# Where VectorE takes the reciprocals of the previous half slot's second side in a chain of four attention layers

## The chip, the core and the metric

The program runs on one core of one Trainium2 chip. TensorE (PE in the rows) multiplies matrices, VectorE (DVE) and ScalarE (ACT) read and write both memories, GpSimd (POOL) works on SBUF, SyncE (SP) issues transfers; each engine runs its own queue in order and waits on semaphores. The metric is the device time of one execution in microseconds, the median of the runs.

## What is computed

Four cross attention layers one after the other on x (8 batches of 128 tokens, 128 channels), with a context of 8 x 128 x 256. Layers 0 and 3 are narrow (16 heads of 8 channels, 4 key heads, an RMS norm ahead of the queries), layers 1 and 2 are wide (16 heads of 64 channels, a column bias on the scores). The reference, cut to what matters:

```python
def narrow(x, cond, wq, wk, wv, wo, norm_w):
    xn = rmsnorm(x, norm_w)
    q = (xn @ wq).reshape(B, T, 16, 8)
    k, v = (cond @ wk).reshape(B, S, 4, 8), (cond @ wv).reshape(B, S, 4, 8)
    ...
    attn = jax.nn.softmax(scores, axis=-1)
    return x + out @ wo

def wide(x, ctx, Wq, Wk, Wv, Wo, bo, ...):
    logits = jnp.einsum('bhqd,bhkd->bhqk', q, k) * scale + col_bias
    probs = jax.nn.softmax(logits, axis=-1)
    ...
    return out @ Wo + bo + x

x = narrow(x); x = wide(x); x = wide(x); x = narrow(x)
```

## The kernel before

**Jobs and half slots.** A job is one layer of one batch: 32 jobs, in the order of `JOBS` (line 73), all four layers for batches 0 to 3 and then for batches 4 to 7. So jobs 0 to 3, 12 to 19 and 28 to 31 are narrow, the others wide. A job has 16 heads in two octets; octet o = 2n + h is half h of job n, and half slot o (`half(n, h)` on each engine) is the turn of each engine's program in which octet o's scores are made. An octet has two sides of four heads, each side one PSUM bank of 128 x 512. There are 64 octets, o = 0 to 63, and a few slots of draining. Each engine's program is unrolled by hand, and only its own order and the semaphores decide when something runs.

**The way of an octet.** TensorE makes the scores of both sides (`scores`, L825 narrow, L836 wide). VectorE's `scores_out(o, side)` (L615) takes each head's column out of PSUM into `probs` and its negated maximum into `negmax`, four heads a side, and signals `scores_read[side]` with the last. ScalarE's `exponentials` (L482) makes the exponentials of the four heads and their row sums and signals `exps_made[side]`. VectorE's `inverse_sums(o, side)` (L622) takes the reciprocals of the four row sums, 128 x 4, and signals `inv_made[side]`. GpSimd's `normalise(o, side)` (L379) multiplies `probs` by them, 128 x 512. One half slot later or more TensorE transposes the side (`transpose_probs(o - 2)` in slot o, L849), VectorE or ScalarE copies the transposes to `probsT` (L626, L499), and TensorE multiplies with the values (`weighted_values`, L870 narrow, L882 wide). Then come the output projection (L900) and the addition to x (L641, L643).

**VectorE's slot o** is, in this order: the addition to x and the mean of squares (odd slots, where due), `scores_out(o, 0)`, `inverse_sums(o - 1, 1)`, `scores_out(o, 1)`, `outputs_out` (L631, L633), `narrow_queries` (L594 and L598, once a narrow job, in even slots there), the copies of octet o - 2's transposes, `inverse_sums(o, 0)`. The reciprocals of octet o's second side thus come one slot late.

**GpSimd's slot o** is `normalise(o, 0)`, `normalise(o, 1)`, and in even slots round narrow jobs, behind these, `narrow_values` (L356), `inverse_root` (L361, the 1/sqrt of the RMS norm of the next narrow job, `inv_rms`), `square` (L373), and `diagonal_keys` (L343) of a job two ahead, at some places with `split_keys` (L328, L331) ahead of it. VectorE's `scores_out(2n, 0)` of a narrow job n waits for `inverse_root(n)` by the semaphore `rms_made`, besides the scores themselves.

**TensorE's slot o**: `scores(o)`, `weighted_values(o - 3)` for a wide job, `transpose_probs(o - 2)`, `weighted_values(o - 3)` for a narrow one, the pieces of the key and value projections that `FILLS` (line 85) gives to the slot (L701 to L703; the last in slot 55), the queries of a job ahead (L788, L796), the mean of squares (L807) and the output projection. Transposes of octet o wait for `pt_read` of octet o - 1.

Of the kernel before, what the change touches and what calls it, by code (L numbers as in the profile page):

```python
# [112 lines left out]
def job(n):  # L113

    return JOBS[n] if 0 <= n < NJOBS else (None, None)


def is_narrow(n):

    return 0 <= n < NJOBS and JOBS[n][0] in NARROW  # L120


def is_wide(n):

    return 0 <= n < NJOBS and JOBS[n][0] not in NARROW
# [7 lines left out]
def scores_bank(o):  # L133

    return "fill" if o >= LAST_FILL + 2 and o % 2 == 1 else "scores"
# [7 lines left out]
def query_half(n):  # L143

    return 2 * n - 3 if n >= 2 and is_narrow(n - 1) else 2 * n - 2


def narrow_index(n):

    return NARROW_JOBS.index(n)  # L150


def build(nc, xT, ctxT, narrow_w, narrow_kv, kv_w, qo_w, small, tokens, outT):
    with ExitStack() as ctx:
# [109 lines left out]
        def valid(o):  # L264

            return 0 <= o < 2 * NJOBS

        def scalar_copy(o):

            return valid(o) and is_narrow(o // 2)  # L270
# [255 lines left out]
        def _(dve):  # L526
# [8 lines left out]
            def norm_weights(n):  # L535

                dve.wait_ge(narrow_q_loaded[n], 16)
                wq = wn[:, NQ + n * REP * STACK:NQ + (n + 1) * REP * STACK]
                nc.vector.tensor_scalar(wq, wq, vec[:, n:n + 1], None, ALU.mult).then_inc(norms_folded, 1)

            def match_tokens():

                dve.wait_ge(tokens_loaded, 16)
                setup(nc.vector.tensor_copy(tok_f[:, :, 0:2], tok_i[:]))

                setup(nc.vector.tensor_scalar(tok_f[:, :, 2:4], tok_f[:, :, 0:2], float(S), None, ALU.add))
                setup(nc.vector.tensor_scalar(tok_f[:], tok_f[:], key_index, None, ALU.is_equal))
                setup(nc.vector.tensor_reduce(hits[:].rearrange("p l m -> p (l m)"), tok_f[:], mybir.AxisListType.X, ALU.max))
                setup(nc.vector.tensor_scalar(only_a[:], hits[:, :, 1], -1.0, 1.0, ALU.mult, ALU.add))
                setup(nc.vector.tensor_tensor(only_a[:], only_a[:], hits[:, :, 0], ALU.mult))  # L550
                for j in range(4):
                    on = hits[:, j, 1:2] if j < 2 else only_a[:, j - 2:j - 1]
                    nc.vector.tensor_scalar(diagonals[:, j, :], identity, on, None, ALU.mult).then_inc(diagonals_made, 1)
# [14 lines left out]
            def split_piece(i):  # L568

                dve.wait_ge(piece_hi, i + 1)  # L570
                nc.vector.tensor_tensor(w_lo[:, i], piece_in[i], w_hi[:, i].bitcast(F32),
                                        ALU.subtract).then_inc(piece_lo[0 if i < 4 else 2], 1)
# [10 lines left out]
            def mean_out(n):  # L583

                dve.wait_ge(ms_full, narrow_index(n) + 1)
                nc.vector.tensor_scalar(rms[:, n % 2:n % 2 + 1], ms_ps[:, 0:1], EPS, None, ALU.add  # L586
                                        ).then_inc(rms_out, 1)

            def narrow_queries(n):

                use = narrow_index(n) + 1
                dve.wait_ge(q_full, uses(n, 0))
                all_parts = qn[0:STACK, n % 2].rearrange("p r t -> p (r t)")
                nc.vector.tensor_scalar(all_parts, q_ps[0:STACK, :], -NARROW_SCALE, None, ALU.mult).then_inc(qn_hi_made, 1)  # L594
                dve.wait_ge(qn_hi_made, use)
                low = slice(PART, 2 * PART)
                rest = qn[low, n % 2].rearrange("p r t -> p (r t)")
                nc.vector.scalar_tensor_tensor(  # L598
                    out=rest, in0=q_ps[low, :], scalar=-NARROW_SCALE, in1=rest.bitcast(F32),
                    op0=ALU.mult, op1=ALU.subtract).then_inc(qn_lo_made, 1)  # L600
                dve.wait_ge(qn_lo_made, use)
                dve.sem_inc(q_read, 1)

            def scores_out(o, side):

                n, h = o // 2, o % 2
                l, b = job(n)
                bias = no_bias[:].broadcast_to([P, S]) if l in NARROW else col_bias[:, l - 1, :]
                scale = inv_rms[:, n % 2:n % 2 + 1] if l in NARROW else 1.0
                if l in NARROW and h == 0 and side == 0:  # L610
                    dve.wait_ge(rms_made, narrow_index(n) + 1)
                dve.wait_ge(scores_full[side], o + 1)
                for q in range(4):
                    cols = slice(q * S, (q + 1) * S)
                    last = nc.vector.tensor_tensor_reduce(  # L615
                        out=probs[:, o % PROBS_RING, side, cols], in0=banks[scores_bank(o)][side][:, cols], in1=bias, scale=scale,
                        scalar=HUGE, op0=ALU.add, op1=ALU.min, accum_out=negmax[:, o % 2, side, q:q + 1])
                last.then_inc(scores_read[side], 1)

            def inverse_sums(o, side):  # L620
                dve.wait_ge(exps_made[side], o + 1)
                nc.vector.reciprocal(inv[:, o % 2, side, :], rowsum[:, o % 2, side, :]).then_inc(inv_made[side], 1)  # L622

            def transposes_out(o, side):
                dve.wait_ge(pt_full[side], o + 1)
                nc.vector.tensor_copy(probsT[:, o % PROBST_RING, side, :], pt_ps[side][:]).then_inc(pt_read[side], 1)  # L626

            def outputs_out(n, h):
                dve.wait_ge(v_full, uses(n, h))
                if is_narrow(n):  # L630
                    nc.vector.tensor_copy(oT[:, 0, :], v_ps[:, 0:T]).then_inc(v_read, 1)  # L631
                else:
                    nc.vector.tensor_copy(oT[:, 4 * h:4 * h + 4, :], v_ps[:].rearrange("p (c q) -> p c q", c=4)  # L633
                                          ).then_inc(v_read, 1)

            def add_input(n):

                l, b = job(n)
                dve.wait_ge(y_full, n + 1)
                if l in NARROW:  # L640
                    ins = nc.vector.tensor_tensor(x[:, b, :], y_ps, x[:, b, :], ALU.add)  # L641
                else:
                    ins = nc.vector.scalar_tensor_tensor(out=x[:, b, :], in0=y_ps, scalar=vec[:, l + 1:l + 2],  # L643
                                                         in1=x[:, b, :], op0=ALU.add, op1=ALU.add)
                ins.then_inc(y_read, 1)

            def half(n, h):
                o = 2 * n + h
                if h == 1 and n >= 2:
                    add_input(n - 2)  # L650
                if h == 1 and is_narrow(n + 1):
                    mean_out(n + 1)
                if valid(o):
                    scores_out(o, 0)
                if valid(o - 1):
                    inverse_sums(o - 1, 1)
                if valid(o):
                    scores_out(o, 1)
                if valid(o - 3) and (h == 0 or is_wide(n - 1)):
                    outputs_out((o - 3) // 2, (o - 3) % 2)  # L660
                for m in NARROW_JOBS:
                    if m > 0 and query_half(m) == o - 1:
                        narrow_queries(m)
                if valid(o - 2):
                    transposes_out(o - 2, 0)
                    if not scalar_copy(o - 2):
                        transposes_out(o - 2, 1)
                if o == 0:
                    split_piece(0)
                if valid(o):  # L670
                    inverse_sums(o, 0)
                if o in (0, 1, 2):
                    split_piece(o + 1)
                if o == 3:
                    match_tokens()
                if o == 4:
                    norm_weights(1)
                if o == 5:
                    column_bias()
                if o in (6, 7):  # L680
                    split_piece(o)
# [11 lines left out]
            for n, h in HALVES:  # L693
                half(n, h)
# [306 lines left out]
```

## Time and profile before

| | |
|---|---|
| median of 3 runs | 382.14 us (380.76 to 382.78) |
| profiled execution | 380.89 us, of which the span on the core is 379.1 |
| mean granted TensorE clock | 0.986 of 2.4 GHz |
| TensorE matmul busy | 359.7 us, 95% |
| VectorE busy | 267.7 us, 71% |
| ScalarE busy | 279.0 us, 74% |
| GpSimd busy | 187.6 us, 49% |

Times inside the program are counted in us from the span's start. The profiled execution has 1.8 us around its span. The shares are an average over stretches that differ: in some TensorE never stops, in others it waits.

### The profile page before, as it was taken

How to read it: one execution, taken by the hardware profiler on the slowest of the kernel's cores; microseconds unless marked ns; L12 is line 12 of the kernel's file. 1: busy time of each engine (PE TensorE's matmuls, PEld its weight loads, DVE VectorE, ACT ScalarE, POOL GpSimd, SP SyncE). 2: the span in 40 equal slices, each digit the busy share in tenths (PEclk: the TensorE clock that was granted, in tenths of full speed). 3: DMA queues.
4: the chain of work that ended last, by engine and by line, in shares of the span. 5: the costliest groups of instructions: out<-in, count | busy, mean ns of one | idle time of the engine just before them, and what ended most of it. 6: DMA issues, size and time to landing. Idle time of an engine off the chain costs nothing.

```text
span 379.1 us, 10494 instructions
## 1 busy us (share of the span) xinstructions
PE 359.7 (95%) x3522; PEld 319.1 (84%) x3522; DVE 267.7 (71%) x1401; ACT 279.0 (74%) x1176; POOL 187.6 (49%) x220
## 2 busy tenths in 40 slices
PE   8889999999999999999999999999999999978665
PEld 8787799899999998889889988888999989867554
DVE  2999975636536547696978886577564785699982
ACT  4889998865665567475899999998566865647793
POOL 3677853733223236454676765443333435447662
PEclk9899999999999999999999999999999999999979
DMA  7925000000000000000000000000000000000000
GB/s 232 411 66 216 1 3 3 2 3 2 1 2 3 2 0 3 2 3 0 10 3 9 9 8 2 3 3 2 0 3 2 3 2 1 2 3 3 7 9 14
DMA packets 4883, 9.91 MB, mean 26 GB/s; under 512 B 608, under 2 KB 3296, under 8 KB 4576
## 3 DMA queue, kind: packets, MB, share of 16 engines
q1 hardware_dynamic: 4400, 8.91, 6.5%
q8 instruction: 29, 0.48, 0.5%
q10 hardware_dynamic: 432, 0.34, 0.4%
q14 instruction: 22, 0.18, 0.2%
HBM read 8.73 MB, written 0.52 MB: 24 GB/s over the span
## 4 chain that ended last, share of the span: by engine, by line
PE 74%; DVE 21%; ACT 3%; issue 1%; DVEq 0%; POOL 0%; POOLq 0%
PE pt_ps L849 13%; PE scores_ps L836 9%; DVE probs L615 8%; PE q_ps L796 8%; PE fill_ps L701 7%; PE v_ps L900 7%; PE v_ps L882 7%; PE fill_ps L702 7%; PE fill_ps L703 7%; PE v_ps L870 3%; DVE probsT L626 3%; ACT probs L482 3%; PE q_ps L788 2%; DVE qn L598 2%; DVE qn L594 2%; PE scores_ps L825 2%
## 5 line engine op out<-in xcount | busy, mean ns | idle before, releaser
L482 ACT ACTIVATE probs<-probs,negmax 128x128 f32<-128x128 f32 x512 | 198.5, 391 | 81.0 <-DVE negmax L615 80.9
L379 POOL TENSOR_TENSOR probs<-probs,inv 128x512 f32<-128x512 f32 x128 | 137.3, 1075 | 176.8 <-DVE inv L622 176.4
L482 ACT ACTIVATION_READ_ACCUMULATOR probs<-probs,negmax 128x1 f32 x512 | 96.8, 189 | 0.0
L615 DVE CUSTOM_DVE_ANT_0 probs<-scores_ps,col_bias 128x128 f32<-128x128 f32 x256 | 58.2, 284 | 39.1 <-PE scores_ps L836 39.1
L849 PE MATMUL pt_ps<-smalls,probs 128*128 128x128 f32 x512 | 70.5, 282 | 6.2 <-DVE probsT L626 6.2
L849 PEld LDWEIGHTS pt_ps<-smalls,probs 128*128 128x128 f32 x512 | 57.6, 143 | 18.2 <-issue 14.8
L615 DVE CUSTOM_DVE_ANT_0 probs<-scores_ps,no_bias,inv_rms 128x128 f32<-128x128 f32 x224 | 64.2, 343 | 5.8 <-PE scores_ps L825 5.4
L626 DVE COPY probsT<-pt_ps 128x512 f32<-128x512 f32 x96 | 63.0, 684 | 2.6 <-PE pt_ps L849 0.5
L615 DVE DVE_READ_ACCUMULATOR2_ANT negmax<- 128x1 f32 x512 | 42.5, 83 | 0.0
L701 PE MATMUL fill_ps<-c_hi,w_hi 128*128 128x256 f32 x128 | 38.3, 300 | 0.0
L836 PE MATMUL scores_ps<-kT,qT 64*128 64x128 f32 x512 | 37.2, 285 | 0.0
L882 PE MATMUL v_ps<-probsT,v 128*64 128x128 f32 x512 | 35.0, 279 | 1.6 <-DVE rms L586 1.0
L702 PE MATMUL fill_ps<-c_hi,w_lo 128*128 128x256 f32 x128 | 36.1, 282 | 0.0
L703 PE MATMUL fill_ps<-c_lo,w_hi 128*128 128x256 f32 x128 | 36.0, 281 | 0.0
L836 PEld LDWEIGHTS scores_ps<-kT,qT 64*128 64x128 f32 x512 | 31.1, 187 | 3.9
L796 PE MATMUL q_ps<-x,w_qo 128*128 128x128 f32 x256 | 34.0, 276 | 0.0
L882 PEld LDWEIGHTS v_ps<-probsT,v 128*64 128x64 f32 x512 | 27.4, 136 | 7.1 <-issue 4.0
L796 PEld LDWEIGHTS q_ps<-x,w_qo 128*128 128x128 f32 x256 | 31.9, 191 | 1.3 <-issue 0.4
L900 PE MATMUL v_ps<-oT,w_qo 128*128 128x128 f32 x256 | 31.7, 277 | 0.0
L643 DVE SCALAR_TENSOR_TENSOR x<-v_ps,smalls,x 128x128 f32<-128x128 f32 x16 | 5.6, 347 | 35.3 <-PE v_ps L900 35.3
L900 PEld LDWEIGHTS v_ps<-oT,w_qo 128*128 128x128 f32 x256 | 29.9, 192 | 0.0
L701 PE MATMUL fill_ps<-w_hi,c_hi 128*128 128x512 f32 x64 | 27.5, 430 | 0.3 <-ACT v L468 0.3
(92 smaller groups left out, 583.2 us busy)
## 6 DMA issues: line engine op xcount, KB each, us to landing
kT<-in_kv_w SPq DMA_DIRECT2D x6, 512.0 KB, 6.4
w_qo<-in_qo_w SPq DMA_DIRECT2D x2, 1024.0 KB, 8.3
v<-in_ctxT SPq DMA_DIRECT2D x4, 256.0 KB, 9.5
v<-in_kv_w SPq DMA_DIRECT2D x2, 512.0 KB, 11.2
outT<-x SPq DMA_DIRECT2D x8, 64.0 KB, 1.6
wn<-in_narrow_w SPq DMA_DIRECT2D x2, 192.0 KB, 5.7
x<-in_xT SPq DMA_DIRECT2D x1, 384.0 KB, 8.1
oT<-in_narrow_kv ACTq DMA_DIRECT2D x1, 256.0 KB, 3.9
```

The lines of the kernel that those rows point to most:

```text
L379: nc.gpsimd.tensor_tensor(p4, p4, inv[:, o % 2, side, :].unsqueeze(2).broadcast_to([P, 4, S]), ALU.mult,).then_inc(probs_made[side], 1)
L482: last = nc.scalar.activation(e, e, ACT.Exp, scale=-1.0, bias=negmax[:, o % 2, side, q:q + 1], accum_out=rowsum[:, o % 2, side, q:q + 1])
L615: last = nc.vector.tensor_tensor_reduce(out=probs[:, o % PROBS_RING, side, cols], in0=banks[scores_bank(o)][side][:, cols], in1=bias, scal ...
L626: nc.vector.tensor_copy(probsT[:, o % PROBST_RING, side, :], pt_ps[side][:]).then_inc(pt_read[side], 1)
L701: nc.tensor.matmul(out, a_hi, b_hi, start=(n == 0), stop=False)
L702: nc.tensor.matmul(out, a_lo, b_hi, start=False, stop=False)
L703: last = nc.tensor.matmul(out, a_hi, b_lo, start=False, stop=(n == len(moving) - 1))
L796: last = nc.tensor.matmul(q_ps[:, c * T:(c + 1) * T], w_qo[:, l - 1, first:first + P], x[:, b, :], start=True, stop=True)
L836: last = nc.tensor.matmul(out[side][:, c * S:(c + 1) * S], qT[rows, 4 * h + c, :], kT[rows, f % KV_RING, 4 * h + c, b % 2 * S:(b % 2 + 1) ...
L849: last = nc.tensor.transpose(pt_ps[side][:, cols], probs[:, o % PROBS_RING, side, cols], identity)
L882: last = nc.tensor.matmul(v_ps[side * WIDE_D:(side + 1) * WIDE_D, c * T:(c + 1) * T], v[:, f % KV_RING, b % 2, head * WIDE_D:(head + 1) * ...
L900: last = nc.tensor.matmul(y_ps, w, oT[:, c, :], start=(c == 0), stop=(c == (1 if l in NARROW else IC) - 1))
```

## The change

In VectorE's `half(n, h)` the call `inverse_sums(o - 1, 1)` moves from ahead of `scores_out(o, 1)` to behind it, in every half slot. Nothing else is different: the same instructions, the same semaphores, and the queues of the other engines as they were.

```diff
@@ -652,10 +652,10 @@
                     mean_out(n + 1)
                 if valid(o):
                     scores_out(o, 0)
+                if valid(o):
+                    scores_out(o, 1)
                 if valid(o - 1):
                     inverse_sums(o - 1, 1)
-                if valid(o):
-                    scores_out(o, 1)
                 if valid(o - 3) and (h == 0 or is_wide(n - 1)):
                     outputs_out((o - 3) // 2, (o - 3) % 2)
```

First place, VectorE in half slots 59 and 60 (narrow jobs 29 and 30), before. `fill_ps0` and `fill_ps1` are the two sides of octet 59's scores, `scores_ps0` and `scores_ps1` those of octet 60; a side has four pairs of rows like the two that stand for it, of which the first alone is shown.

```order
L615 ISA probs,negmax<-fill_ps0,no_bias,inv_rms 128x128 [waits scores_full_0]
...
L622 RECIPROCAL inv<-rowsum 128x4 [waits exps_made_1]
L615 ISA probs,negmax<-fill_ps1,no_bias,inv_rms 128x128 [waits scores_full_1]
...
L626 COPY probsT<-pt_ps0 128x512 [waits pt_full_0]
L622 RECIPROCAL inv<-rowsum 128x4 [waits exps_made_0]
L615 ISA probs,negmax<-scores_ps0,no_bias,inv_rms 128x128 [waits scores_full_0,rms_made]
...
L622 RECIPROCAL inv<-rowsum 128x4 [waits exps_made_1]
L615 ISA probs,negmax<-scores_ps1,no_bias,inv_rms 128x128 [waits scores_full_1]
...
L631 COPY oT<-v_ps 128x128 [waits v_full]
```

The same stretch, after:

```order
L615 ISA probs,negmax<-fill_ps0,no_bias,inv_rms 128x128 [waits scores_full_0]
...
L615 ISA probs,negmax<-fill_ps1,no_bias,inv_rms 128x128 [waits scores_full_1]
...
L622 RECIPROCAL inv<-rowsum 128x4 [waits exps_made_1]
L626 COPY probsT<-pt_ps0 128x512 [waits pt_full_0]
L622 RECIPROCAL inv<-rowsum 128x4 [waits exps_made_0]
L615 ISA probs,negmax<-scores_ps0,no_bias,inv_rms 128x128 [waits scores_full_0,rms_made]
...
L615 ISA probs,negmax<-scores_ps1,no_bias,inv_rms 128x128 [waits scores_full_1]
...
L622 RECIPROCAL inv<-rowsum 128x4 [waits exps_made_1]
L631 COPY oT<-v_ps 128x128 [waits v_full]
```

The reciprocal that waits for `exps_made_1` moved past the four heads of the slot's second side, in both slots.

Second place, VectorE in half slot 28 (narrow job 14), the end of the slot, before, from the last row of its first side:

```order
L615 ISA negmax 128x1
L622 RECIPROCAL inv<-rowsum 128x4 [waits exps_made_1]
L615 ISA probs,negmax<-scores_ps1,no_bias,inv_rms 128x128 [waits scores_full_1]
...
L631 COPY oT<-v_ps 128x128 [waits v_full]
L594 TENSOR_SCALAR qn<-q_ps 96x512 [waits q_full]
L598 SCALAR_TENSOR_TENSOR qn<-q_ps,qn 32x512 [waits qn_hi_made]
L626 COPY probsT<-pt_ps0 128x512 [waits qn_lo_made,pt_full_0]
```

and after:

```order
L615 ISA negmax 128x1
L615 ISA probs,negmax<-scores_ps1,no_bias,inv_rms 128x128 [waits scores_full_1]
...
L622 RECIPROCAL inv<-rowsum 128x4 [waits exps_made_1]
L631 COPY oT<-v_ps 128x128 [waits v_full]
L594 TENSOR_SCALAR qn<-q_ps 96x512 [waits q_full]
L598 SCALAR_TENSOR_TENSOR qn<-q_ps,qn 32x512 [waits qn_hi_made]
L626 COPY probsT<-pt_ps0 128x512 [waits qn_lo_made,pt_full_0]
```

Here too the reciprocal moved by one side, to just ahead of the copies that end the slot.

## Rows read from the trace of the kernel before

**Rows 1.** The page's part 1: busy time of each engine.

```profile
PE 359.7 (95%) x3522; PEld 319.1 (84%) x3522; DVE 267.7 (71%) x1401; ACT 279.0 (74%) x1176; POOL 187.6 (49%) x220
```

**Rows 2.** Page's part 4: the chain that ended last, by engine.

```profile
PE 74%; DVE 21%; ACT 3%; issue 1%; DVEq 0%; POOL 0%; POOLq 0%
```

**Rows 3.** Waits: who waited for whom, us in total, times, longest.

```profile
PE pt_ps L849 <- DVE probsT L626: 6.2, 8, 2.0
DVE inv L622 <- ACT probs L482: 5.5, 8, 1.8
```

**Rows 4.** Busy time by stretch: length, then PE, PEld, DVE, ACT, POOL, PEclk.

```profile
47.00:151.00 104.00, 104.00 (x1057) 94.51 (x1056) 61.26 (x340) 73.74 (x306) 41.23 (x41) 1.00 0.01 2
...
178.00:227.00 49.00, 48.50 (x464) 42.68 (x463) 41.16 (x222) 43.17 (x185) 33.22 (x45) 1.00 0.03 7
...
242.00:325.00 83.00, 83.00 (x898) 75.15 (x898) 55.68 (x319) 60.43 (x267) 32.59 (x34) 1.00 0.01 2
```

**Rows 5.** VectorE in order of time, slots 59 and 60: start, duration, instruction [idle before].

```profile
350.62 0.35 DVE L615 CUSTOM_DVE_ANT_0 probs<-fill_ps,no_bias,inv_rms 128x128 f32<-128x128 f32 x1
...
350.89 0.18 DVE L622 RECIPROCAL inv<-rowsum 128x4 f32<-128x4 f32 x1
350.98 0.33 DVE L615 CUSTOM_DVE_ANT_0 probs<-fill_ps,no_bias,inv_rms 128x128 f32<-128x128 f32 x1
...
352.88 0.35 DVE L615 CUSTOM_DVE_ANT_0 probs<-scores_ps,no_bias,inv_rms 128x128 f32<-128x128 f32 x1
...
354.71 0.18 DVE L622 RECIPROCAL inv<-rowsum 128x4 f32<-128x4 f32 x1 [0.66 <-ACT probs L482]
...
355.87 0.29 DVE L631 COPY oT<-v_ps 128x128 f32<-128x128 f32 x1
```

**Rows 6.** GpSimd in order of time, octet 58's second side and what follows.

```profile
351.14 1.04 POOL L379 TENSOR_TENSOR probs<-probs,inv 128x512 f32<-128x512 f32 x1 [0.57 <-DVE inv L622]
...
352.29 0.55 POOL L361 TENSOR_TENSOR inv_rms<-rms,half_power 128x1 f32<-128x1 f32 x1
```

**Rows 7.** GpSimd in order of time, the inverse root for job 14.

```profile
181.87 0.55 POOL L361 TENSOR_TENSOR inv_rms<-rms,half_power 128x1 f32<-128x1 f32 x1
```

**Rows 8.** VectorE in order of time, slot 28.

```profile
183.04 0.35 DVE L615 CUSTOM_DVE_ANT_0 probs<-scores_ps,no_bias,inv_rms 128x128 f32<-128x128 f32 x1 [0.58 <-PE scores_ps L825]
...
185.45 0.28 DVE L631 COPY oT<-v_ps 128x128 f32<-128x128 f32 x1
```

**Rows 9.** TensorE in order of time, slot 29, the transposes of octet 27.

```profile
188.04 0.52 PE L849 MATMUL pt_ps<-smalls,probs 128*128 128x128 f32 x3 [0.50 <-DVE probsT L626]
```

**Rows 10.** GpSimd in order of time, the inverse root for job 17.

```profile
210.10 0.56 POOL L361 TENSOR_TENSOR inv_rms<-rms,half_power 128x1 f32<-128x1 f32 x1
```

**Rows 11.** VectorE in order of time, the start of slot 34.

```profile
211.32 0.35 DVE L615 CUSTOM_DVE_ANT_0 probs<-scores_ps,no_bias,inv_rms 128x128 f32<-128x128 f32 x1 [0.64 <-PE scores_ps L825]
```

**Rows 12.** TensorE in order of time, slots 61 to 64.

```profile
358.45 1.94 PE L849 MATMUL pt_ps<-smalls,probs 128*128 128x128 f32 x8 [1.03 <-DVE probsT L626]
...
361.73 1.94 PE L849 MATMUL pt_ps<-smalls,probs 128*128 128x128 f32 x8 [0.49 <-DVE probsT L626]
363.60 1.79 PE L870 MATMUL v_ps<-probsT,v_narrow 128*32 128x128 f32 x32
...
369.66 1.06 PE L849 MATMUL pt_ps<-smalls,probs 128*128 128x128 f32 x8 [2.00 <-DVE probsT L626]
370.65 1.08 PE L870 MATMUL v_ps<-probsT,v_narrow 128*32 128x128 f32 x32
```

**Rows 13.** GpSimd in order of time, octet 62's second side.

```profile
367.93 1.04 POOL L379 TENSOR_TENSOR probs<-probs,inv 128x512 f32<-128x512 f32 x1 [0.36 <-DVE inv L622]
```

**Rows 14.** GpSimd in order of time, octet 0: first and second side.

```profile
15.08 1.93 POOL L379 TENSOR_TENSOR probs<-probs,inv 128x512 f32<-128x512 f32 x1 [2.30 <-DVE inv L622]
17.43 1.04 POOL L379 TENSOR_TENSOR probs<-probs,inv 128x512 f32<-128x512 f32 x1 [0.42 <-DVE inv L622]
```

**Rows 15.** Busy time by stretch, columns as in Rows 4.

```profile
358.00:365.00 7.00, 6.06 (x46) 4.95 (x50) 6.10 (x40) 5.37 (x28) 4.82 (x6) 0.52 0.03 9
```

## The prediction

> **What bounds the kernel now.** I read the page's busy shares first, then the chain of waits, then busy time by stretch, and last the three engines in order of time at the places that these pointed to. TensorE is busy for 95% of the span [rows 1], and the chain that ended last runs through it for 74%, through VectorE for 21% and through ScalarE for 3% [rows 2]. The stretches tell where that is so: between 47 and 151 us and between 242 and 325 us matmuls fill the whole time, and between 178 and 227 us 48.5 of 49 us [rows 4]. There nothing that VectorE or GpSimd does some tenths sooner or later counts, so long as TensorE finds its inputs. The rest, the first 47 us, the passage from wide to narrow, a wait round 188 us and the last 50 us, is where VectorE sets the pace.
>
> What the change aims at is small. VectorE waits for ScalarE's exponentials ahead of a reciprocal 8 times, 5.5 us in all, the longest 1.8 us [rows 3]. That longest one is in slot 64, where no maxima are left to put ahead of it. Three are like the one of slot 60, 0.66 us [rows 5]: slots 38, 60 and 62. The others are a tenth or so, as in slot 28, or belong to first sides.
>
> **The change, part by part.** *The work.* Nothing is added or removed: 64 reciprocals move past four column maxima each, with no DMA among what moves and no other queue touched. The maxima follow one another at 0.27 us (350.62 to 350.89), and a reciprocal takes 0.09 us of that rhythm (350.89 to 350.98) [rows 5]. So a moved reciprocal runs 4 x 0.27 = 1.08 us later, the second side's maxima 0.09 us earlier, and all that follows at the same time, if nobody waited. The 0.09 us are worth nothing: ScalarE takes the second side's exponentials behind the first side's, and isn't held by them.
>
> *Who waits for the reciprocals.* GpSimd's second normalisation starts 0.25 us after the reciprocal starts (350.89 to 351.14) [rows 5, 6], so it moves by 1.08 us as well. Its direct reader, the transposes, comes in the next slot but one, and in the wide layers far later than 1.08 us. But GpSimd works in order, and in even slots of the narrow layers the values' copy, the inverse root, the square and the diagonal keys stand behind it. The inverse root of the next narrow job is what the first maxima of slot 2n wait for. That is the term that the diff doesn't show. The reciprocals of octet 2n - 2 run in slot 2n - 1, the root follows, and slot 2n's first maxima follow that.
>
> *Slot 60.* Now the root ends at 352.29 + 0.55 = 352.84 [rows 6], and the first maxima start at 352.88 [rows 5], 0.04 us behind, so there is no room (slots 38 and 62 read alike). With the change the root ends at 353.92 and the maxima start at 353.96. VectorE then runs both sides without a stop, 8 x 0.27 = 2.16 us, takes the reciprocals at 356.12 and starts the output copy 0.09 us later, at 356.21. Now it starts at 355.87 [rows 5]. So the wait of 0.66 us for ScalarE is gone, a new one of 1.08 us for GpSimd stands ahead of the slot, and the sum, with the 0.09 us, is a loss: **+0.34 us**. From there the copies of transposes that TensorE waits for follow one another on VectorE, so it reaches TensorE.
>
> *Slot 62* moves more: its root stands behind slot 61's reciprocals, already 0.34 us late, so its maxima start 1.08 + 0.34 us later than now. But in that slot VectorE's output copy waits for TensorE's weighted values, which start at 363.60 and take 1.79 us [rows 12]. Both sides fit ahead of that, with about 0.4 us to spare, so I take 0, with 0.4 us as the upper bound.
>
> *Slot 28.* The root ends at 182.42 [rows 7], the maxima start at 183.04, held by the scores [rows 8]. That room of 0.62 us is less than 1.08: the root would end at 183.50, the maxima start at 183.54, the output copy at 183.54 + 2.16 + 0.09 = 185.79, where it is now at 185.45 [rows 8]. **+0.34 us** again, and again on the path: TensorE stands idle for 0.50 us until VectorE's copy of transposes comes, at 188.04 [rows 9]. Behind it TensorE is the bound, which doesn't give time back.
>
> *Slots 32, 34, 36 and 38.* In slot 34 the root ends at 210.66 [rows 10] and the maxima start at 211.32, so they are held to 211.78, 0.46 us later. VectorE was idle for 0.64 us here [rows 11], and TensorE is full in this stretch [rows 4]. The cover of the copies of transposes that TensorE wants next is this: between 178 and 227 us TensorE stood idle for 0.5 us in all, which is the one wait ahead of octet 27's transposes [rows 4, 9], so it has not had to wait for VectorE in these slots. Cost 0; I allow 0.2 us in all for a cover that is thinner than the 0.34 us by which the slot's later work moves.
>
> *The end.* Octet 62's second normalisation now runs from 367.93 to 368.97 [rows 13]; with 1.08 + 0.34 us it ends at 370.39. TensorE starts that octet's transposes at 369.66 and reaches the second side four of eight later, about 370.1; with 0.34 us, about 370.5 [rows 12]. It just fits: 0 to 0.1 us, and the same at two other second sides with little room (octets 4 and 36). I take **+0.1 us** for all of them.
>
> *The first 47 us.* GpSimd's late chain grows here too, but it has more than 1.08 us of room wherever VectorE or TensorE reads from it; 0. One thing about GpSimd's durations is seen: octet 0's first normalisation took 1.93 us, its second 1.04 [rows 14]; the first ran while VectorE subtracted pieces out of two SBUF operands. The moved second side of octet 5 comes beside such a subtraction, and would take 0.9 us longer. It has that room. The Trainium skill, "GPSIMD Engine Reference", section 8, says that GpSimd shares its SBUF interfaces with VectorE and contends with instructions with two SBUF inputs; by that rule the 0.9 us are to be expected, by a flat 1.04 us they are not, and the sum is the same either way.
>
> *Sum:* 0.34 + 0.34 + 0.1 = 0.8 us. The span of 379.1 becomes 379.9, the profiled execution of 380.89 becomes 381.7, and the median, 1.25 us above that execution, 382.14 + 0.8 = **382.9 us**.
>
> **The rivals.** *A: a small gain.* If the root is not what holds slot 60 (VectorE's own previous reciprocal ends at about the same moment as the root, so the row can't tell the two apart), and if GpSimd has its input earlier than I think, the 0.66 us of slot 60 come free, and at most those of slot 62: -0.7 to -1.3 us, 381.4 to 380.8. Against it: the wait is in the program, and 1.08 us of delay don't vanish whoever holds the slot now.
>
> *B: slower, by TensorE's clock.* Between 358 and 365 us the granted clock was 0.52 on average, mostly the lower level of 1.2 GHz [rows 15]; just ahead of it TensorE had waited 1.03 us for a copy of VectorE's [rows 12]. At that level the eight transposes took 1.94 us and the weighted values 1.79; at 2.4 GHz 1.06 and 1.08 [rows 12]. The change lengthens the idle time ahead of slot 61 by 0.34 us. If the low clock takes in one more such pair on the path, that is 0.88 + 0.71 = 1.6 us, and with the 0.8 and the 0.2 of the thin covers 2.6 us: 384.7. It decides from the point where TensorE's stop before slot 61 is long enough to bring the fall forward or hold back the rise. Against it: 0.34 us is little beside the idle time that is there already. [...]
>
> *C: nothing.* TensorE's work hides slot 28, and slot 60's loss is taken up by the later waits, the 2.00 us ahead of 369.66 among them [rows 12]: 382.1. Against it: that wait is for VectorE itself, whose stream is what is late.
>
> **How the numbers follow.** The forecast gets 0.60, A 0.12, B 0.13, C 0.15. A change under 0.5%, 1.9 us, is about what a measurement of this kernel can't tell from none; the runs themselves lie 2 us apart. The forecast, A and C lie within that, B doesn't. With the spread of a median laid on top: faster by over 0.5% 0.08, within 0.74, slower 0.18. The range goes from A's lower end to B's, 380.8 to 384.7.
>
> **What would show it.** In the trace of after: VectorE's waits for ScalarE ahead of reciprocals fall from 5.5 us to about 3; the first maxima of slots 28, 32 to 38, 60 and 62 start 0.03 to 0.05 us behind the end of an inverse root, half a us to 1.4 us later against their slot than now; TensorE's idle time ahead of octet 27's transposes grows from 0.50 to about 0.84 us; the wide stretches are unchanged to 0.1 us. I'd be wrong if the first maxima of slot 60 started ahead of 353.5 us (after allowing for what the program is late by then), if the root turned out to be ready long before them, if the wide stretches moved at all, or if the low clock covered another stretch than between 358 and 365 us.

## The result, and the profile after

| | before | after |
|---|---|---|
| median of 5 runs | 381.36 us (380.76 to 382.78) | 386.12 us (384.95 to 386.34) |
| profiled execution, its span | 380.89, 379.1 us | 386.15, 384.4 us |
| mean granted TensorE clock | 0.986 | 0.975 |

The changed kernel is slower: the ratio is 1.0111, 95% interval 1.0082 to 1.0140. That is 4.2 us (3.1 to 5.3), where 0.8 us were forecast, and its time lies above the upper end of the range on record, 384.7 us. The page of after, busy times and chain by engine, against [rows 1, 2]:

```profile
PE 362.6 (94%) x3522; PEld 320.5 (83%) x3522; DVE 269.3 (70%) x1401; ACT 279.8 (73%) x1176; POOL 187.4 (49%) x220
...
PE 70%; DVE 21%; issue 4%; POOL 2%; ACT 1%; DMA 1%; ACTq 0%; DVEq 0%; POOLq 0%
```

TensorE is busy 2.9 us longer with the same 3522 matmuls, and GpSimd, which had no share of the chain, now has 2%. The waits of after (who for whom, us in all, times, longest), against [rows 3]:

```profile
DVE probs L615 <- POOL inv_rms L361: 8.8, 8, 1.1
PE pt_ps L849 <- DVE probsT L626: 6.8, 8, 1.8
DVE inv L622 <- ACT probs L482: 3.3, 4, 1.8
```

The reciprocals wait for ScalarE 2.2 us less, as foretold, and VectorE's maxima wait 8.8 us for the inverse root, about 1.1 us each in slots 28, 30, 32, 34, 36, 38, 60 and 62, a wait that was in no row of before. The wide stretch of [rows 4], moved by what the kernel is late by then, is as full as it was:

```profile
48.50:152.50 104.00, 104.00 (x1057) 94.50 (x1057) 61.74 (x342) 73.75 (x306) 41.82 (x42) 1.00 0.01 2
```

**The two places of the sum.** In slot 28 the root (GpSimd in order of time) and the maxima (VectorE), after:

```profile
184.62 0.55 POOL L361 TENSOR_TENSOR inv_rms<-rms,half_power 128x1 f32<-128x1 f32 x1
```
```profile
185.21 0.35 DVE L615 CUSTOM_DVE_ANT_0 probs<-scores_ps,no_bias,inv_rms 128x128 f32<-128x128 f32 x1 [1.10 <-POOL inv_rms L361]
...
187.39 0.17 DVE L622 RECIPROCAL inv<-rowsum 128x4 f32<-128x4 f32 x1
```

The maxima start 0.04 us behind the root's end (185.17), both sides run without a stop, and the reciprocals follow 2.18 us later. TensorE's wait ahead of octet 27's transposes, 0.50 us in [rows 9], is 0.84:

```profile
190.04 0.41 PE L849 MATMUL pt_ps<-smalls,probs 128*128 128x128 f32 x2 [0.84 <-DVE probsT L626]
```

Slot 60 reads like slot 28: maxima at 356.07, 0.04 us behind the root, again 1.10 us of waiting.

**Where the time went.** I took the start of the same instruction in both traces (a slot's first maxima on VectorE) and set slot 3's to zero, since the input transfers let a program start a few tenths sooner or later. In us against before; "last" is the last addition to x; the ratios of the later rows are against runs of before on the same chip:

| kernel | slot 4 | slot 8 | slot 29 | slot 59 | slot 61 | slot 63 | last | ratio of times |
|---|---|---|---|---|---|---|---|---|
| after | 0.63 | 1.44 | 1.78 | 1.89 | 2.23 | 2.31 | 5.04 | 1.0111 |
| e1, slots 0 to 7 moved | 0.64 | 1.50 | 1.49 | 1.47 | 1.46 | 1.21 | 2.93 | 1.0055 |
| e2, slots 8 to 57 moved | 0.01 | 0.00 | 0.34 | 0.44 | 0.45 | 1.07 | 2.80 | 1.0016 |
| e3, slots 58 on moved | 0.01 | 0.01 | 0.00 | -0.01 | 0.34 | 0.42 | 3.14 | 1.0037 |
| e4, norm_weights in slot 12 | 0.64 | 0.44 | 0.79 | 0.89 | 1.23 | 0.82 | 2.10 | 1.0065 |
| e5, root first | 0.36 | 1.37 | 1.21 | 1.21 | 0.41 | -0.03 | 1.69 | 1.0025 |
| e6, before, root first | 0.43 | 1.75 | 1.75 | 1.71 | 1.71 | 1.45 | 3.17 | 1.0035 |
| e7, after, tail filled | 0.63 | 1.64 | 1.97 | 2.06 | 2.39 | 1.97 | 2.15 | 1.0068 |
| e8, before, tail filled | 0.00 | -0.01 | -0.02 | -0.06 | -0.07 | -0.83 | -0.63 | 1.0002 |
| e9, before, norm_weights in slot 12 | 0.01 | 1.55 | 1.54 | 1.51 | 1.51 | 0.76 | 3.86 | 1.0032 |
| e10, after, slot 3 as before | 0.54 | 1.38 | 1.73 | 1.80 | 2.14 | 2.27 | 2.30 | 1.0080 |
| e11, after, slots 3 and 4 as before | 0.55 | 0.55 | 0.89 | 0.97 | 1.30 | 1.94 | 3.66 | 1.0071 |
| e12, what it points to | 0.00 | 0.00 | -0.18 | -0.28 | -1.07 | -2.28 | -1.91 | 0.9947 |

After loses 1.44 us by slot 8, 0.34 us in slot 28, 0.34 us in slot 60, 0.2 us in small steps, and 2.7 us behind slot 63's maxima. Up to slot 61 the same order gave the same shift within 0.1 us from trace to trace, with one exception: e7 is 0.2 us later at slot 8 than after, and its granted clock between 37 and 47 us was 0.83 where that of after was 1.00.

**The first loss** is in slots 3 and 4, in instructions of VectorE that I had given no thought. Before, VectorE in order of time, its setup work in slots 3 to 5, then GpSimd in the same time:

```profile
30.60 1.02 DVE L547 TENSOR_SCALAR tok_f<-tok_f,smalls 128x16 f32<-128x16 f32 x1
...
31.86 0.69 DVE L549 TENSOR_SCALAR only_a<-hits 128x2 f32<-128x2 f32 x1
32.58 0.16 DVE L550 TENSOR_TENSOR only_a<-only_a,hits 128x2 f32<-128x2 f32 x1
32.78 0.48 DVE L553 TENSOR_SCALAR qT<-smalls,hits 128x128 f32<-128x128 f32 x2
...
38.36 0.39 DVE L539 TENSOR_SCALAR wn<-wn,smalls 128x384 f32<-128x384 f32 x1
```
```profile
30.49 1.04 POOL L343 TENSOR_TENSOR kd<-kn,smalls 96x512 fp32r<-96x512 f32 x1
31.49 1.04 POOL L379 TENSOR_TENSOR probs<-probs,inv 128x512 f32<-128x512 f32 x1
...
35.90 2.38 POOL L386 TENSOR_TENSOR w_lo<-v,w_hi 128x1024 fp32r<-128x1024 f32 x1
```

and after, the same two views:

```profile
31.08 0.23 DVE L547 TENSOR_SCALAR tok_f<-tok_f,smalls 128x16 f32<-128x16 f32 x1
...
31.56 0.31 DVE L549 TENSOR_SCALAR only_a<-hits 128x2 f32<-128x2 f32 x1
31.90 1.01 DVE L550 TENSOR_TENSOR only_a<-only_a,hits 128x2 f32<-128x2 f32 x1
32.94 1.16 DVE L553 TENSOR_SCALAR qT<-smalls,hits 128x128 f32<-128x128 f32 x2
...
39.21 1.22 DVE L539 TENSOR_SCALAR wn<-wn,smalls 128x384 f32<-128x384 f32 x1
```
```profile
31.79 1.04 POOL L343 TENSOR_TENSOR kd<-kn,smalls 96x512 fp32r<-96x512 f32 x1
32.79 1.04 POOL L379 TENSOR_TENSOR probs<-probs,inv 128x512 f32<-128x512 f32 x1
...
37.83 2.37 POOL L386 TENSOR_TENSOR w_lo<-v,w_hi 128x1024 fp32r<-128x1024 f32 x1
```

Compare ends. L547, an operation on 128x16 numbers, takes 0.23 us in one trace and 1.02 in the other, where it ends at 31.62, just behind GpSimd's instruction that ends at 31.53. After, L550 ends at 32.91 behind GpSimd's 32.83, the first pair of L553 at 34.10 behind 33.83, and L539 at 40.43 behind GpSimd's 40.20: it started 1.38 us into that instruction and stood until it was over, then took 0.23 us more. The change made all of these GpSimd instructions later, so others of VectorE's fall into them, and in this stretch VectorE sets the pace. The setup instructions of slot 3 (L544 to L553) together take 0.62 us longer than before, some longer and some shorter, which is what slot 4 is late by; L539 with its 0.83 us more makes it 1.46 at slot 5. Not every pair collides: in before VectorE's reduction L548 started at 31.65, inside GpSimd's instruction of 31.49 to 32.53, and took its 0.17 us; in after L547 ran from 31.08 to 31.31 inside GpSimd's inverse root of 128x1 (30.92 to 31.47).

**The loss at the end** is, in these two traces, the clock. TensorE after, in order of time, against [rows 12], and busy time by stretch with the granted clock behind POOL, against [rows 15]:

```profile
364.18 1.10 PE L849 MATMUL pt_ps<-smalls,probs 128*128 128x128 f32 x8 [1.76 <-DVE probsT L626]
365.22 1.81 PE L870 MATMUL v_ps<-probsT,v_narrow 128*32 128x128 f32 x32
...
372.19 1.94 PE L849 MATMUL pt_ps<-smalls,probs 128*128 128x128 f32 x8 [0.98 <-DVE probsT L626]
374.06 1.83 PE L870 MATMUL v_ps<-probsT,v_narrow 128*32 128x128 f32 x32
...
378.95 1.89 PE L870 MATMUL v_ps<-probsT,v_narrow 128*32 128x128 f32 x32 [0.89 <-ACT probsT L499]
381.23 0.80 PE L900 MATMUL v_ps<-oT,wn 128*128 128x128 f32 x2 [0.39 <-DVE oT L631]
```
```profile
365.20:375.50 10.30, 8.50 (x81) 6.92 (x84) 6.75 (x41) 8.72 (x40) 6.30 (x8) 0.51 0.03 8
375.50:378.90 3.40, 1.94 (x22) 1.20 (x14) 1.86 (x4) 0.60 (x1) 0.00 (x0) 0.98 0.07 19
378.90:384.40 5.50, 2.69 (x34) 1.97 (x34) 0.58 (x2) 0.00 (x0) 0.00 (x0) 0.51 0.04 12
```

The lower level of 1.2 GHz covers 10 us where it covered 7, and comes back for the last 5.5 us. Slot 64's transposes and values, 1.06 and 1.08 us before, take 1.94 and 1.83: 1.63 us more. The last values and projection take 1.89 and 0.80 us, in the trace of before 1.08 and 0.49: 1.1 us more. Together 2.7 us, all that is lost behind slot 63. These are two single executions; how much is low differs from one execution to the next in every kernel here, the old order included (e2, with the old order in its tail, lost 2.4 us behind slot 61 in its profiled execution and 0.2 by its ratio). But all five executions of after had a mean clock of 0.973 to 0.977. Among the 89 executions of before that were timed beside the experiments, the 9 with 0.975 or less took 382.9 us on average, the 49 with 0.986 381.0, the 12 with 0.995 or more 380.5; the other 19, in between, took 382.4, so not all of the spread follows the mean clock.

### The profile page after: what moved, and what is told of

It is laid out like the page before. It is cut to its first block, busy times and chain, and to the rows that moved or that the text cites. A ratio compares the mean times of both kernels' runs of the same rounds, so it can differ in the third digit from the quotient of the medians.

```text
span 384.4 us, 10494 instructions
## 1 busy us (share of the span) xinstructions
PE 362.6 (94%) x3522; PEld 320.5 (83%) x3522; DVE 269.3 (70%) x1401; ACT 279.8 (73%) x1176; POOL 187.4 (49%) x220
## 4 chain that ended last, share of the span: by engine, by line
PE 70%; DVE 21%; issue 4%; POOL 2%; ACT 1%; DMA 1%; ACTq 0%; DVEq 0%; POOLq 0%
PE pt_ps L849 12%; PE scores_ps L836 9%; DVE probs L615 9%; PE q_ps L796 8%; PE fill_ps L701 7%; PE v_ps L900 7%; PE v_ps L882 7%; PE fill_ps L702 7%; PE fill_ps L703 7%; PE v_ps L870 3%; DVE probsT L626 3%; DVE qn L598 2%; PE q_ps L788 2%; DVE qn L594 2%; PE scores_ps L825 2%
## 5 line engine op out<-in xcount | busy, mean ns | idle before, releaser
L379 POOL TENSOR_TENSOR probs<-probs,inv 128x512 f32<-128x512 f32 x128 | 135.6, 1062 | 179.5 <-DVE inv L622 178.7
L615 DVE CUSTOM_DVE_ANT_0 probs<-scores_ps,col_bias 128x128 f32<-128x128 f32 x256 | 56.6, 287 | 39.1 <-PE scores_ps L836 39.1
L615 DVE CUSTOM_DVE_ANT_0 probs<-scores_ps,no_bias,inv_rms 128x128 f32<-128x128 f32 x224 | 63.0, 347 | 11.0 <-POOL inv_rms L361 8.8
```

The costliest lines, as they stand in the source:

```text
L379: nc.gpsimd.tensor_tensor(p4, p4, inv[:, o % 2, side, :].unsqueeze(2).broadcast_to([P, 4, S]), ALU.mult,).then_inc(probs_made[side], 1)
L615: last = nc.vector.tensor_tensor_reduce(out=probs[:, o % PROBS_RING, side, cols], in0=banks[scores_bank(o)][side][:, cols], in1=bias, scal ...
```

## The experiments

**Which slots.** Three kernels with the moved order in a part of the slots:

```diff
-                if valid(o - 1):
+                late = o < 8
+                if valid(o - 1) and not late:
                     inverse_sums(o - 1, 1)
                 if valid(o):
                     scores_out(o, 1)
+                if valid(o - 1) and late:
+                    inverse_sums(o - 1, 1)
```

> The reciprocals of the second side stand behind the second side's maxima in half slots 0 to 7 alone, and ahead of them, as before, from slot 8 on. Theory 1 (the loss is a sum of places, and the largest that I had missed is in the first 47 us, where VectorE's short SBUF instructions meet GpSimd's later ones): slots 4 to 8 come 1.4 to 1.5 us later than before, every wide slot behind them by the same, and the time grows by 1.5 us, whatever the tail adds. Theory 2 (the loss is TensorE's clock in the tail, and the shift of 1.5 us that the trace of after shows at slot 8 is an accident of one execution): slot 8 comes within 0.3 us of before, and the time is that of before.

Measured 1.0055 (1.0025 to 1.0085), and 1.50 us late at slot 8 (slot 4 only 0.64): theory 1. Half of the loss by the ratios is in eight slots in which I had booked nothing.

The same with `8 <= o < 58`:

> The moved order in half slots 8 to 57 alone. Theory 1: octet 27's transposes come 0.34 us later against before, nothing else up to slot 57 adds over 0.1 us, and the time grows by 0.4 us. Theory 2: the same shift of 0.3 to 0.4 us in the middle, and a time that goes with the low clock in the tail: 0.4 us alone if that covers the same slots as before, 1 to 3 us more if not.

Measured 1.0016 (0.9988 to 1.0043), 0.34 us at slot 29 and 0.44 at slot 59. And with `o >= 58`:

> The moved order from half slot 58 on alone. Theory 1: up to slot 58 the trace is that of before; slot 60's output copy comes 0.34 us later and slot 62's another 0.1 us at most; the time grows by 0.4 to 0.5 us if the clock falls where it fell before. Theory 2: the longer stops of TensorE in slots 60 to 64 bring a longer stretch at the low clock: 1.5 to 3 us on top, 2 to 3.5 us in all.

Measured 1.0037 (1.0011 to 1.0064): 0.34 us at slot 61, 0.42 at slot 63, as worked out, and 2.7 us more by the last addition in its profiled execution. The three excesses add up to 1.0108, the whole change measured 1.0111, which fits a sum of places, though each ratio is known to 0.3% only. By the ratio the tail costs 1.4 us (0.4 to 2.4), of which 0.4 us are VectorE's: more than theory 1 gave, less than theory 2.

**The lengthened instructions.** The changed kernel with its longest one moved out of the way:

```diff
-                if o == 4:
+                if o == 12:
                     norm_weights(1)
```

> The changed kernel, with VectorE's norm_weights(1) (a multiplication of SBUF by a vector, L539) in half slot 12 instead of slot 4, where GpSimd idles. Theory 1 (that instruction took 1.22 us rather than 0.39 since it ran into GpSimd's split_piece, which now comes later): slot 5 comes 1.2 us earlier than in the changed kernel, 0.83 for the lost overlap and 0.39 for its own time, of which 0.3 stand in VectorE's stream, so 1.1 to 1.2 us; L539 in slot 12 takes 0.3 to 0.4 us, hidden behind TensorE; the time falls by 1.1 to 1.2 us against the changed kernel. Rival (the 1.22 us belong to the instruction's place in VectorE's queue, not to GpSimd): it takes over 1 us in slot 12 too, or slot 5 comes no earlier.

Slot 5 comes 1.15 us earlier than in after, as foretold, slot 8 1.00 us earlier, and the ratio falls to 1.0065 (1.0033 to 1.0097), 1.8 us where 1.1 to 1.2 were foretold, a difference within the intervals. In slot 12, where it starts while GpSimd is idle, 0.16 us ahead of its next instruction, VectorE's row is

```profile
82.23 0.39 DVE L539 TENSOR_SCALAR wn<-wn,smalls 128x384 f32<-128x384 f32 x1
```

The control, the same edit on the kernel before:

> The kernel before with norm_weights(1) in half slot 12 instead of slot 4. Theory 1 (L539 runs free of GpSimd in slot 4 of the kernel before, 0.39 us): slot 5 comes 0.3 us earlier and no more, against 1.0 in the changed kernel, and the time falls by 0.3 us at most. Rival (L539 costs over 1 us in slot 4 in any kernel): 1 us.

Measured 1.0032 (1.0005 to 1.0058), so slower, where I expected a small gain. Slot 5 did come 0.32 us earlier. But that brought VectorE's next small instruction ahead to a moment 0.09 us behind the start of GpSimd's second `split_piece`; VectorE and GpSimd in order of time in this kernel:

```profile
42.00 2.36 DVE L558 TENSOR_SCALAR suppress<-smalls 128x2 f32<-128x2 f32 x1
```
```profile
41.91 2.43 POOL L386 TENSOR_TENSOR w_lo<-v,w_hi 128x1024 fp32r<-128x1024 f32 x1
```

Two numbers a partition took 2.36 us, from 42.00 to 44.36; GpSimd's instruction ended at 44.34. In the kernel before it takes 0.14 us, and starts one hundredth of a us ahead of GpSimd's; the same two views of before:

```profile
41.91 0.14 DVE L558 TENSOR_SCALAR suppress<-smalls 128x2 f32<-128x2 f32 x1
```
```profile
41.92 2.41 POOL L386 TENSOR_TENSOR w_lo<-v,w_hi 128x1024 fp32r<-128x1024 f32 x1
```

This is the clearest pair of rows of the study: for these two instructions not the work but who starts first decides, and the later one stands until the other is done. The Trainium skill, "SBUF — State Buffer", section "Who interferes with whom", says just this: VectorE and GpSimd share a pair of SBUF ports under an exclusive lock, copies, casts and tensor_scalar on SBUF may take it as well as instructions with two SBUF inputs, and issue order decides who blocks. The rows agree (0.14 against 2.36 us). That the moved maxima and the output copies, which read PSUM, kept their 0.32 to 0.35 and 0.26 to 0.29 us beside any GpSimd instruction agrees too.

The other half, slot 3 (the lines are against e1's kernel):

```diff
-                late = o < 8
+                late = o != 3
```

> The changed kernel with the old order in half slot 3 alone, so that octet 2's second normalisation, and octet 3's first behind it, come when they came before. Theory 1 (the 0.63 us that slot 4 is late are VectorE's token and diagonal instructions running into these two of GpSimd): slot 4 starts within 0.1 us of before, and L539 in slot 4 still takes over 1.1 us, since slot 4's reciprocals are still late; slot 8 comes 0.8 to 1.1 us later than before instead of 1.44. Rival (VectorE's maxima of slot 4 wait for something else that is late): slot 4 still comes 0.6 us late.

Slot 4 is still 0.54 us late and slot 8 1.38, so this expectation failed, 4 runs at 1.0080 (1.0049 to 1.0111). VectorE's row of slot 3 and GpSimd's show why:

```profile
30.29 1.50 DVE L547 TENSOR_SCALAR tok_f<-tok_f,smalls 128x16 f32<-128x16 f32 x1
```
```profile
30.73 1.04 POOL L343 TENSOR_TENSOR kd<-kn,smalls 96x512 fp32r<-96x512 f32 x1
```

GpSimd is late already out of slot 2: there its diagonal keys started at 25.74, 0.09 us behind a subtraction of VectorE's with both operands in SBUF (L571, 25.65 to 26.85), and took 2.00 us; in before they came first, at 24.96, and took 1.04. So now L547 (0.23 us when free) stands from 30.29 to 31.79, until the diagonal keys of the next slot end at 31.77. Undoing one slot swaps one overlap for another. With both slots undone:

> The changed kernel with the old order in half slots 3 and 4. Theory 1: no instruction of VectorE in SBUF alone is lengthened by GpSimd more than before, L539 takes 0.39 us, slot 8 comes within 0.2 us of before, and the time falls by 1.3 to 1.6 us against the changed kernel, to 0.6 to 0.8 per cent above before. Rival (the two places are only part, slots 0 to 2 and 5 to 7 give the rest): slot 8 is still over 0.5 us late.

L539 takes 0.39 us and the 0.9 us of slot 4 are gone, but slot 3's 0.55 us stay, for the same reason (L547 takes 1.50 us again); the bound of 0.2 us was missed. Ratio 1.0071 (1.0040 to 1.0102). So slot 4's loss was taken away by an edit aimed at it (e4, e11), slot 3's went whole only where all of slots 0 to 7 were left as before (e2, e12); which overlaps it is made of rests on the rows.

**The root.** The changed kernel with the inverse root freed from the late reciprocals:

```diff
                 if valid(o):
                     normalise(o, 0)
+                for n in NARROW_JOBS:
+                    if o == 2 * n - 2 and n > 0:
+                        inverse_root(n)
+                if valid(o):
                     normalise(o, 1)
                 for n in NARROW_JOBS:
-                    if o == 2 * n - 2 and n > 0:
-                        inverse_root(n)
```

> The changed kernel with GpSimd's inverse_root ahead of normalise(o, 1) instead of behind it, so that the maxima of a narrow job no longer stand behind the late reciprocals. Theory 1 (the new wait for the root is what slots 28, 60 and 62 lose by): slot 28's first maxima start with the scores again, octet 27's transposes come 0.1 to 0.2 us earlier than before the change instead of 0.34 later; slot 60's output copy comes some 0.8 us earlier than before the change instead of 0.34 later, since the 0.66 us of waiting for ScalarE are then really covered; 1.5 to 1.8 us in all against the changed kernel, the clock aside; the first 47 us stay as slow as in the changed kernel. Rival (the root was no bound, the maxima are late for another reason): slots 28 and 60 start as in the changed kernel, and the time is that of the changed kernel.

Between slots 8 and 29 it gains 0.16 us where after loses 0.34, between 59 and 61 it gains 0.80 us where after loses 0.34, both as worked out. VectorE in slot 60: both sides without a stop, no wait for ScalarE and none for GpSimd.

```profile
353.75 0.35 DVE L617 CUSTOM_DVE_ANT_0 probs<-scores_ps,no_bias,inv_rms 128x128 f32<-128x128 f32 x1
...
355.92 0.17 DVE L624 RECIPROCAL inv<-rowsum 128x4 f32<-128x4 f32 x1
```

The ratio is 1.0025 (1.0001 to 1.0048), 3.3 us below that of after, where 1.5 to 1.8 us were foretold with the clock aside: the traces explain 0.5 us in slot 28 and 1.14 in slot 60. The first slots keep it above 1. The same edit on the kernel before:

> The kernel before with GpSimd's inverse_root ahead of normalise(o, 1), nothing else. Theory 1: the root ended 0.04 us ahead of the maxima of slots 38, 60 and 62, which VectorE's own queue held to the same moment, so it gives 0 to 0.1 us a slot; in all within 0.3 us of before. Rival (the root did hold these slots before too): slots 38, 60 and 62 start over 0.2 us earlier, and the time falls by 0.3 to 0.6 us.

Slots 38, 60 and 62 don't move by 0.1 us against their neighbours: the root held next to nothing there. Yet the ratio is 1.0035 (1.0015 to 1.0056), not within 0.3 us of before, because slot 8 is 1.75 us late: with GpSimd's small instruction elsewhere, a cast of 128x8 in slot 3 (L544, line 546 in this kernel) takes 1.98 us, from 30.14 to 32.12, across two GpSimd instructions in a row (30.05 to 31.08 and 31.05 to 32.08), and L558 (line 560 in this kernel) takes 1.93 us.

```profile
30.14 1.98 DVE L546 CAST tok_f<-tok_i 128x8 f32<-128x8 int32 x1
...
42.36 1.93 DVE L560 TENSOR_SCALAR suppress<-smalls 128x2 f32<-128x2 f32 x1
```

**The clock.** Matmuls that nobody reads, in TensorE's idle time of slots 60 to 64, into a bank of scores that has been read:

```diff
+            def keep_clock(o, count):
+                pe.wait_ge(scores_read[0], o)
+                spare = banks[scores_bank(o - 1)][0][:, 0:T]
+                for _ in range(count):
+                    nc.tensor.matmul(spare, mean_w[:], mean_w[:], start=True, stop=True)
...
                 if valid(o):
                     scores(n, h)
+                if 60 <= o <= 64:
+                    keep_clock(o, 4)
...
+                if o == 60:
+                    keep_clock(o, 6)
```

> The changed kernel with 26 matmuls of 128x128 more on TensorE, whose result nobody reads: four each in half slots 60 to 64 ahead of the transposes and six in slot 60 ahead of the mean of squares, in its idle time there, into a bank of scores that has been read. Theory 1 (1.6 to 2.8 us of the tail are the low clock): the granted clock stays at 2.4 GHz to about 375 us, the transposes and weighted values of slots 62 to 64 take 1.06 to 1.08 us each, and the time falls by 1 to 2.5 us against the changed kernel. Rival (the tail is bound by VectorE and ScalarE whatever the clock): the time falls by under 0.3 us, or grows by what the matmuls take, up to 1 us.

TensorE in slot 64 and slot 65 of this kernel:

```profile
371.32 1.25 PE L849 MATMUL pt_ps<-smalls,probs 128*128 128x128 f32 x8 [0.22 <-DVE probsT L626]
372.51 1.08 PE L870 MATMUL v_ps<-probsT,v_narrow 128*32 128x128 f32 x32
...
376.64 1.08 PE L870 MATMUL v_ps<-probsT,v_narrow 128*32 128x128 f32 x32 [0.89 <-ACT probsT L499]
```

The clock holds to 378 us, behind the last weighted values, which take 1.08 us, and from slot 63 to the last addition the kernel loses 0.2 us on before instead of 2.7. The ratio is 1.0068 (1.0044 to 1.0092) against 1.0111: 1.6 us less, give or take 1.4, and the mean clock of the eight executions is 0.988 to 0.995. On the kernel before:

> The kernel before with the same 26 matmuls. Theory 1: its one low stretch, 358 to 365 us, costs 0.7 us on the path, since VectorE's maxima of slot 62 end 0.7 us ahead of the weighted values that it waits for; the time falls by 0.5 to 1 us, less than in the changed kernel, so the clock is part of what separates the two. Rival: it falls by as much as in the changed kernel, and the clock has no part in the difference.

The profiled execution is 0.63 us better at the end and its slot 63 0.83 us earlier, as worked out, but the ratio is 1.0002 (0.9976 to 1.0027): over many executions the matmuls give the kernel before nothing that can be told, where 0.5 to 1 us were foretold. So by these ratios the low clock costs the changed kernel about 1.7 us more than the one before, with an interval of about 1.7 us to either side, which just reaches zero. The other way round, with the matmuls in both kernels the change costs 2.5 us by the ratios and 2.8 us in the two traces (2.15 and -0.63 in the table; 0.2 of them are e7's low clock ahead of slot 8), where without them it costs 4.2 by the ratio: this is what is left when the clock holds. In this pair slot 62 costs its own 0.34 us (2.46 us between the kernels at slot 61, 2.80 at slot 63). The 0.1 us that after shows there hides it, since in the profiled execution of before the low clock of 358 to 365 us had made slots 61 and 62 slow as well.

The other kernels give a second reading of that. Take from each ratio's excess, times 381 us, what the kernel is late at slot 61 in the table; what is left belongs to the last slots. With the moved order in the tail it is 2.0 (after), 1.1 (e3), 1.2 (e4), 0.5 (e5, root first), 0.9 (e10) and 1.4 us (e11); with the old order there 0.6 (e1), 0.2 (e2), -0.4 (e6) and -0.3 us (e9). So the moved order costs about 1 us more behind slot 61, of which slot 62 explains 0.34, and it costs it on the average of many executions. With the matmuls in, what is left is 0.2 us (e7) and 0.1 us (e8). Each of these figures carries the interval of its ratio, about 1 us either way. That the low clock costs the changed kernel time is shown by e7; that it costs it more than the one before is likely by all of these readings together and not proven by one. What in the longer stops (1.60 us ahead of slot 60's mean of squares where before had 1.31, 0.82 ahead of slot 62's projection where before had 0.42) tips the clock was not taken apart, and stays open.

**What it points to.** The moved order from slot 8 on, the root first for jobs from 12 on, and the matmuls of the tail:

> What the study points to: the moved order from half slot 8 on, the inverse root ahead of normalise(o, 1) for jobs from 12 on, and the 26 matmuls of the tail; slots 0 to 7 as before. Theory 1: up to slot 27 as before, octet 27's transposes 0.18 us earlier, slot 60's output copy 0.8 us earlier on top, the low clock gone from the tail: 1.4 to 1.8 us below before, a ratio of 0.995 to 0.996. Rival (gains and clock don't add, the last slots wait for ScalarE anyway): within 0.5 us of before.

Measured 0.9947 (0.9925 to 0.9969), median 378.99 us against 381.13: faster than both kernels. That is 2.0 us, at the upper end of what was foretold or above it. It gains 0.18 us in slot 28 and 0.8 us in slot 60, and nothing is lost ahead of slot 8; its mean clock was 0.991 to 0.999. How the rest divides between the clock and the order was not taken apart.

## Why the prediction was wrong, point by point

- **TensorE bounds the wide stretches.** Right; they didn't move.
- **What the change aims at is small.** Right: the waits of reciprocals for ScalarE fell from 5.5 to 3.3 us, where I said about 3.
- **A moved reciprocal takes GpSimd's root with it, and the maxima wait for it.** Right, and right in size: 1.10 us of waiting in slots 28 and 60, 0.34 us lost in each. e5 undid both losses. Slot 30 waited too, which I had not named; it cost nothing (1.78 us late at slot 29 and at slot 31).
- **Slots 32 to 38: 0.** Right to 0.1 us (slots 29 to 59: 0.11 us).
- **The second sides with little room: 0.1 us.** About right in size; the small steps came to 0.2 us, 0.11 between slots 29 and 59 and 0.08 between 61 and 63, where slot 62 lies; that the 0.11 are these second sides was not shown.
- **Slot 62: 0, at most 0.4 us.** The bound held, the 0 did not: with the clock held in both kernels (e7, e8) it cost 0.34 us.
- **The first 47 us: 0.** This is the step that failed first: a term put at nothing that measured 1.44 us, and 2.1 us (1.0 to 3.2) by e1's ratio. I checked that each late GpSimd result still came ahead of its reader. I did not check which VectorE instructions a later GpSimd instruction would lie on: L550, L553 and L539 took 1.01, 1.16 and 1.22 us beside such ones, where in before they took 0.16, 0.48 and 0.39. I had the rule and a row for it [rows 14], but looked only at GpSimd's side, and only at octet 5's normalisation. Short instructions of VectorE on SBUF that took 1.02 and 0.69 us (L547, L549) stood in the trace of before; free of GpSimd they take 0.23 and 0.17 us (e6).
- **The low clock stays where it is.** This is the second step that failed, worth some 1 to 2 us: in after it covered 365 to 375 us and the last 5.5 us, where in before it covered 358 to 365. Rival B had the mechanism and, with 1.6 us, a price near what was found, but I gave it 0.13, since 0.34 us more idle time seemed little beside what was there. I read the place of the low stretch off one execution as if it were fixed. And in slot 62, where I had VectorE's output copy wait for TensorE's weighted values, TensorE came to wait for the copy: the stop ahead of its projection grew from 0.42 to 0.82 us.
- **Rivals A and C.** Neither: with the root as bound there was no gain, and none of the late work was hidden.
- **The range.** Its upper end, 2.6 us above before, was B on top of the forecast; measured were 4.2 us by the ratio. The 1.44 us of the first slots are about the difference, and they had no bound above zero at all, though a row with 1.93 against 1.04 us lay open [rows 14].

## What to carry to other kernels

When an instruction of one engine moves, ask not only who reads its result but also which instructions on the engine that shares its SBUF ports it will now run beside; list the short SBUF instructions that are unusually long in the trace, since they mark where such overlaps already cost. A wait that sits in an engine's queue ahead of small housekeeping (here the inverse root behind a normalisation) passes its lateness on to whatever waits for the housekeeping: put the housekeeping first. In a draining tail, tenths of idle TensorE time may be paid for a second time through the clock; compare the granted clock over many executions before you trust the place of a low stretch in one.

## What the runs showed that I had not expected

- A VectorE instruction on two numbers a partition took 2.36 us beside a GpSimd instruction of 2.43 us that had started 0.09 us ahead, and 0.14 us when it started 0.01 us ahead of it. One of 128x8 stood 1.98 us across two GpSimd instructions in a row.
- Because of that, edits of a few tenths of a us in the first 47 us made slot 8 of the kernel before 1.5 to 1.75 us later (e6, e9), and the time 1.2 to 1.3 us longer by the ratios: the order of before is a lucky one.
- Reciprocals of 128x4 on SBUF were not lengthened: 128 of them took 161 to 180 ns in the trace of before, 13 of these wholly inside a GpSimd instruction.
- 26 matmuls that nobody reads, put into TensorE's stops at the end (up to 1.8 us each in the changed kernel), took 1.6 us off the changed kernel and nothing measurable off the kernel before.
